# One block table instead of three in a fused attention and expert kernel

## The reference, cut to what matters

```python
# layer 1: attention inside each image, n = 256 positions
q, k, v = wq @ xf + bq, wk @ xf + bk, wv @ xf
sim = softmax(q.T @ k / sqrt(64) + key_mask, axis=2)
x = x + gamma * (sim @ v)
# layer 2: linear attention across the 8 images (cumulative sums over l), on normalized tokens
q, k, v = relu(t @ q_w.T + q_b), relu(t @ k_w.T + k_b), t @ v_w.T + v_b
attn = einsum(q_, cumsum(k_ v)) / max(einsum(q_, cumsum(k_)), 1e-6)
t = t + attn @ out_w.T + out_b
# layer 3: 2048 tokens, 8 experts, each token goes to its best two
probs = softmax(ln(t) @ router_w)          # top 2, weights made to sum to 1
h = silu(x @ w1[e]) * (x @ w3[e])
t = t + sum over the two experts of weight * (h @ w2[e])
```

## Time and profile before

| | us |
|---|---|
| median of 3 runs (lowest, highest) | 198.16 (197.84, 201.89) |
| the profiled execution | 198.26 |
| its span, first to last instruction | 196.5 |
| PE, POOL, DVE, ACT busy | 145.5, 100.4, 100.9, 97.4 |

### The profile page before, as it was taken

The page is one execution under the profiler, slowest core; times in us unless marked ns, Lnnn a source line. Parts: engine busy times, 40 slices in busy tenths (PEclk is TensorE's granted clock), DMA queues, the critical chain, the costliest instruction groups (busy, mean ns, idle before and its releaser), DMA issues.

```text
span 196.5 us, 4178 instructions
## 1 busy us (share of the span) xinstructions
PE 145.5 (74%) x1113; PEld 126.6 (64%) x1113; DVE 100.9 (51%) x400; ACT 97.4 (50%) x294; POOL 100.4 (51%) x142
## 2 busy tenths in 40 slices
PE   1899999999687978763998808866499989892000
PEld 1478886887476756452997808856399979791000
DVE  2177377789329699885156830234045445320163
ACT  3298986878387737131356502433235655552000
POOL 0003340727868688678068777756116746756000
PEclk9999999999969999996699985999889999999555
DMA  6989200000000000139442158661342332110595
GB/s 172 315 251 415 100 2 0 0 3 27 27 29 19 29 27 17 54 96 286 131 126 95 54 142 300 186 203 50 84 95 66 89 77 67 34 42 0 163 273 207
DMA packets 17925, 21.37 MB, mean 109 GB/s; under 512 B 3355, under 2 KB 14304, under 8 KB 17646
## 3 DMA queue, kind: packets, MB, share of 16 engines
q1 hardware_dynamic: 14910, 16.38, 27.8%
q0 software_dynamic: 2272, 4.24, 6.3%
q10 hardware_dynamic: 720, 0.49, 0.9%
HBM read 15.21 MB, written 6.33 MB: 110 GB/s over the span
## 4 chain that ended last, share of the span: by engine, by line
PE 45%; DMA 13%; POOL 12%; issue 11%; SPq 9%; DVE 6%; ACT 2%; POOLq 0%; DVEq 0%; ACTq 0%
PE ps L879 14%; PE ps L894 7%; POOL rows_x L502 6%; DMA xb<-rows_x 4%; PE ps L743 3%; SPq L376 3%; PE ps L723 3%; DMA XT<-rows_y 3%; PE ps L868 2%; DMA rows_x<-pad 2%; PE ps L715 2%; PE ps L708 2%; PE ps L707 2%; PE ps L782 2%; DMA X<-in_x_ch 2%
## 5 line engine op out<-in xcount | busy, mean ns | idle before, releaser
L510 POOL DMA_INDIRECT rows_y<-yb,xb x39 | 38.3, 981 | 27.1 <-ACT yb L661 20.2
L502 POOL DMA_INDIRECT rows_x<-xrow,slot x32 | 36.0, 1125 | 17.8 <-issue 10.8
L879 PE MATMUL ps<-xbT,WB 128*128 128x128 f32 x312 | 42.1, 292 | 0.0
L879 PEld LDWEIGHTS ps<-xbT,WB 128*128 128x128 f32 x312 | 40.6, 210 | 0.0
L894 PE MATMUL ps<-W,hid 128*128 x156 | 25.4, 296 | 5.0 <-DVE hid L1194 3.9
L653 ACT ACTIVATE gate<-ps 128x256 f32<-128x256 f32 x39 | 14.9, 383 | 22.3 <-PE ps L879 19.6
L894 PEld LDWEIGHTS ps<-W,hid 128*128 128x128 f32 x156 | 21.2, 201 | 6.8 <-issue 6.6
L1194 DVE TENSOR_TENSOR hid<-gate,ps 128x256 f32<-128x256 f32 x39 | 16.0, 414 | 18.0 <-ACT gate L653 15.2
L1207 DVE COPY WB<-W 128x512 f32 x22 | 10.2, 462 | 24.5 <-PE ps L879 21.5
L661 ACT ACTIVATE yb<-ps,xb 128x128 f32<-128x128 f32 x39 | 14.4, 368 | 12.6 <-PE ps L894 11.1
L868 PE MATMUL ps<-CF,xb 128*128 128x128 f32 x39 | 9.1, 296 | 11.6 <-DMA xb<-rows_x 10.9
(11 more groups left out here) (141 smaller groups left out, 294.6 us busy)
## 6 DMA issues: line engine op xcount, KB each, us to landing
WB<-in_w SPq DMA_DIRECT2D x17, 256.0 KB, 3.4
xb<-rows_x SPq DMA_DIRECT2D x39, 65.0 KB, 2.0
W<-in_w SPq DMA_DIRECT2D x1, 2048.0 KB, 10.4
X<-in_x_ch SPq DMA_DIRECT2D x8, 128.0 KB, 3.7
XT<-in_x_tok SPq DMA_DIRECT2D x8, 128.0 KB, 3.7
W<-in_w SPq DMA_DIRECT2D x1, 1024.0 KB, 12.5
XT<-rows_y SPq DMA_DIRECT2D x4, 192.0 KB, 4.5
X<-rows_y SPq DMA_DIRECT2D x4, 192.0 KB, 4.6
```

The costliest lines, as they stand in the source:

```text
L502: pool.indirect_dma_start(rows_x, bass.IndirectOffsetOnAxis(ap=slot[:, g:g + 1], axis=0), xrow[:, i * T + t, c, :], None, bounds_check=DUM ...
L510: pool.indirect_dma_start(rows_y, bass.IndirectOffsetOnAxis(ap=xb[:, n, DEST_COL:ROW].bitcast(I32), axis=0), yb[:, n, :], None, bounds_che ...
L879: last = pe.matmul(bank(BANK_GU[s])[:, k * P:(k + 1) * P], WB[:, s % WBS, k * P:(k + 1) * P], xbT[:, s % XBT, :], start=True, stop=True)
```

## The change

- One table of 39 blocks is made after all 8 images are routed. `table_taken`, `pad_lists` and the tables' interleaving go.
- The padding is stored ahead of everything: eight fills of 64 partitions x 8 experts x 520 numbers (1.06 MB each) write every row of all lists. `scatter` of image i waits for fill i.
- `TENSOR_LOAD` of table entries: two at once, of 26 and 13 registers, on each of SP, PE and DVE, ahead of the first block.
- On POOL only the power is left of each norm. The variance plus epsilon (`lin_spread`, `route_spread`) and the negated product (`lin_shift`, `route_shift`) are DVE instructions.
- All 39 blocks' weights are copied by DVE; SP issues no weight loads in the expert part.
- 24 bf16 matmuls of ones on ones stand at the head of PE.
- New written orders on POOL, ACT, PE and DVE: the expert part stands behind all of the front part, and `turn_x`, `gate_up(s + 1)`, `down(s)` alternate singly. New PSUM banks.

```diff
-READ = 8
+READ = 26
+PACK = 4
+WARM_MATMULS = 24
-TABLES = ((4, 9, 0), (6, 8, 9), (8, 22, 17),)
+TABLES = ((8, 39, 0),)
...
+        def read_table(eng, registers, line, k):
+            _, blocks, first = TABLES[k]
+            for s in range(first, first + blocks, READ):
+                m = min(READ, first + blocks - s)
+                eng.reg_load(registers[s:s + m], table[line:line + 1, s:s + m])
...
+            def fill_rows(c):
+                here = rows_x[0:E * CAP, :].rearrange("(e r) d -> e (r d)", e=E)[:, c * N * ROW:(c + 1) * N * ROW]
+                sp.dma_start(here.rearrange("e (p k) -> p e k", k=PACK * ROW),
+                             pad[0:N // PACK, :].unsqueeze(1).broadcast_to([N // PACK, E, PACK * ROW])).then_inc(filled[c], 16)
+            fill_rows(0)
             sp.dma_start(W13[:, :], w13).then_inc(ld_w13, 16)
             sp.dma_start(W2[:, :], w2).then_inc(ld_w13, 16)
+            for c in range(1, B):
+                fill_rows(c)
...
             for k, (_, blocks, first) in enumerate(TABLES):
-                if k == len(TABLES) - 1:
-                    pad_lists()
                 sp.wait_ge(table_done, k + 1)
+                read_table(sp, first_row, T_ROW, k)
...
                 for s in range(first, first + blocks):
                     load_rows(s)
-                    if k < len(TABLES) - 1:
-                        load_weights(s)
...
             def rstd_ffn(i):
                 b = i % 2
-                pool.wait_ge(mv2_done, 2 * (i + 1))
+                pool.wait_ge(ve2_done, i + 1)
                 if i >= 2:
                     pool.wait_ge(xrow_done, 2 * (i - 1))
-                pool.tensor_scalar(nm2[:, b, :], mv2[:, b, :, 0], -1.0, None, ALU.mult)
-                link(pool.tensor_scalar(ve2[:, b, :], mv2[:, b, :, 1], LN_EPS, None, ALU.add))
-                link(pool.tensor_tensor(rs2[:, b, :], ve2[:, b, :], CF[:, C_HALF:C_HALF + T], ALU.pow))
-                pool.tensor_tensor(nb2[:, b, :], nm2[:, b, :], rs2[:, b, :], ALU.mult).then_inc(rs2_done, 1)
+                    pool.wait_ge(nb2_done, i - 1)
+                pool.tensor_tensor(rs2[:, b, :], ve2[:, b, :], CF[:, C_HALF:C_HALF + T], ALU.pow).then_inc(rs2_done, 1)
...
                     pool.wait_ge(dest_ready, 1)
+                    pool.wait_ge(filled[i], 16)
...
+            pe.wait_ge(ones_ready, 1)
+            for _ in range(WARM_MATMULS):
+                pe.matmul(bank(BANK_CV[0])[:, 0:P], ONES[:, :], ONES[:, :], start=True, stop=True)
...
+            def route_spread(i):
+                dv.wait_ge(mv2_done, 2 * (i + 1))
+                dv.tensor_scalar(ve2[:, i % 2, :], mv2[:, i % 2, :, 1], LN_EPS, None, ALU.add).then_inc(ve2_done, 1)
+
+            def route_shift(i):
+                dv.wait_ge(rs2_done, i + 1)
+                if i >= 2:
+                    dv.wait_ge(xrow_done, 2 * (i - 1))
+                dv.scalar_tensor_tensor(out=nb2[:, i % 2, :], in0=mv2[:, i % 2, :, 0], scalar=-1.0, in1=rs2[:, i % 2, :],
+                                        op0=ALU.mult, op1=ALU.mult).then_inc(nb2_done, 1)
```

More of the change, by code:

```diff
@@ L279, in hybrid_block @@
         warm_ready = sem("warm_ready")
-        pool_done = sem("pool_done")
+        ones_ready = sem("ones_ready")
+        filled = [sem(f"filled{c}") for c in range(B)]
+        ve1_done = sem("ve1_done")
+        nb1_done = sem("nb1_done")
+        nb2_done = sem("nb2_done")
         rs1_done = sem("rs1_done")
@@ L358, in pieces @@
             return sum(len(halves(i)) for i in range(n))
-        def table_of(s):
-            return [k for k, (_, _, first) in enumerate(TABLES) if first <= s][-1]
-        def table_reader(eng, line, most):
-            sets = [[eng.alloc_register(f"line{line}_{half}_{n}") for n in range(READ)] for half in range(2)]
-            turn = [1]
-            def read(s):
-                _, blocks, first = TABLES[table_of(s)]
-                n = (s - first) % READ
-                if n == 0:
-                    turn[0] = 1 - turn[0]
-                    m = min(READ, first + blocks - s)
-                    eng.reg_load(sets[turn[0]][0:m], table[line:line + 1, s:s + m])
-                return eng.snap(sets[turn[0]][n], min_val=0, max_val=most)
-            return read
+        def read_table(eng, registers, line, k):
[3 more added lines that the diff above has]
+                eng.reg_load(registers[s:s + m], table[line:line + 1, s:s + m])
         @block.sync
@@ new lines, in _ @@
+            scatter(7, 1); scatter(7, 2); scatter(7, 3); result(0); result(1); result(2); result(3); result(4)
+            result(5); result(6); result(7); result(8); result(9); result(10); result(11); result(12)
+            result(13); result(14); result(15); result(16); result(17); result(18); result(19); result(20)
+            result(21); result(22); result(23); result(24); result(25); result(26); result(27); result(28)
+            result(29); result(30); result(31); result(32); result(33); result(34); result(35); result(36)
@@ L527, in _ @@
+            result(37); result(38)
         @block.scalar
@@ new lines, in _ @@
+            turn_x(21); gate_up(19); down(18); turn_x(22); gate_up(20); down(19); turn_x(23); gate_up(21)
+            down(20); turn_x(24); turn_x(25); gate_up(22); down(21); turn_x(26); gate_up(23); down(22)
+            turn_x(27); gate_up(24); down(23); turn_x(28); gate_up(25); down(24); turn_x(29); gate_up(26)
+            down(25); turn_x(30); gate_up(27); down(26); turn_x(31); turn_x(32); gate_up(28); down(27)
+            turn_x(33); gate_up(29); down(28); turn_x(34); gate_up(30); down(29); turn_x(35); gate_up(31)
@@ L935, in _ @@
+            down(30); turn_x(36); gate_up(32); down(31); turn_x(37); gate_up(33); down(32); turn_x(38)
+            gate_up(34); down(33); gate_up(35); down(34); gate_up(36); down(35); gate_up(37); down(36)
+            gate_up(38); down(37); down(38)
         @block.vector
@@ L1142, in table_rows @@
                 dv.wait_ge(cnt_done, k + 1)
-                if last:
-                    dv.tensor_tensor(pad_row[:, :], cnt[0:1, :], CF[0:1, C_ECAP:C_ECAP + E], ALU.add).then_inc(pad_row_done, 1)
                 link(dv.tensor_scalar(up[:, :], cnt, float(P - 1) if last else 0.0, None, ALU.add))
@@ new lines, in _ @@
+            table_copy(0); read_experts(0); weights(0); weights(1); weights(2); weights(3); weights(4)
+            weights(5); hidden(0); weights(6); hidden(1); weights(7); hidden(2); weights(8); hidden(3)
+            weights(9); hidden(4); weights(10); hidden(5); weights(11); weights(12); hidden(6); hidden(7)
+            weights(13); hidden(8); weights(14); hidden(9); weights(15); hidden(10); weights(16); hidden(11)
+            weights(17); hidden(12); weights(18); hidden(13); weights(19); hidden(14); weights(20); hidden(15)
@@ L1249, in _ @@
+            hidden(38)
             for q in range(PARTS):
```

354 lines of the change are left out of this document (167 added, 187 removed).

## The result

The changed kernel takes 189.92 us (median of 4 runs, 189.45 to 190.78) beside 198.92 us for the kernel before on the same chip (4 runs, 197.84 to 201.89): ratio 0.957, 95% interval 0.950 to 0.964. A second set of six runs gave 189.32 and 0.944 (0.938 to 0.950). Forecast were 187.5 in a range of 181.0 to 196.5, and faster by over 2%.

A forecast was written before the change was run, and what follows sets the result against it. It took PE to bound the kernel until 50 us and from 146 to 178, POOL's spacing from 50 to 92. Terms: 103.6 (last scatter landed) + 64.4 (expert part) + 17.7 (end) + 1.8 (outside span) = 187.5 us; range 181 to 196.5.

The forecast's parts named there:

- first scatter starts: Front part: POOL's first scatter starts at 45.1 us, where it stood at 44.8 before.
- first to last scatter: Front part on POOL: 55.9 us between these starts, with the last scatter starting at 101.
- landed to end of last `down`: Expert part: 39 blocks on PE, with first rows, low clock and gaps, take 64.4 us after the last landing.
- the warm matmuls: Head of PE: 24 matmuls in idle time shorten the slow pace, saving 1.7 us, at worst nothing.
- the new order: Front part on PE: 14 more records stand ahead of the first ranks, adding 2.0 us.
- two DVE waits: After 52 us: waits of 3.6 and 2.4 us, laid to image 5's power behind four scatters, go: -6.0 us.
- DVE stuck behind powers: Front part: DVE's negated products wait for POOL's powers behind 15 scatters; up to 19 us slower, 206.5; chance 0.07.
- the cover that I named: Front part: seven us of DVE work between image 2's slots and image 4's product, against 5.1 + 0.8 needed.
- Register loads at no cost: Before the expert part: loading 39 registers takes 2.6 to 8.7 us, hidden by scatters and landing; charged nothing, at most 1.0.
- Fills at no cost: Front part: eight padding stores on SP's queue finish by 71 us, hidden; late fills cost 15 us, chance 0.04.
- The clock's 2.0 us: Start of the expert part: PE begins at the lower clock after idling, +1.8 us, with first turns +2.0.
- POOL held up by weight copies: Expert part: each DVE copy keeps POOL out for 0.43 us, results take 1.71 each, total 203; chance 0.04.

The follow-up runs named there:

- the last run: Changed kernel with 8 and 14 extra float32 128x128 matmuls put into PE's waits before the first `gate_up`: 191.40 us, ratio 0.952.

## Why the prediction was right, point by point

**What bounds, and in which order.** Held: three stages, POOL's scatters, then PE, and one valley. The forecast of 187.5 was 2.4 under the measured 189.9; the sum's terms, against the profiled execution:

| term | forecast | measured | off |
|---|---|---|---|
| first scatter starts | 45.1 | 48.99 | +3.9 |
| first to last scatter | 55.9 | 56.0 | +0.1 |
| landing | 2.6 | 2.3 | -0.3 |
| landed to end of last `down` | 64.4 | 63.6 | -0.8 |
| end | 17.7 | 17.3 | -0.4 |
| outside the span | 1.8 | 1.9 | +0.1 |

The 2.6 us of these are the miss against 190.09 (the median, 189.92, is 0.2 lower).

**The term that was mis-sized: the first scatter.** I took -1.7 for the warm matmuls and +2.0 for the new order, +0.3 together. Between the two profiled executions the first scatter moved by +4.2, from 44.79 to 48.99, in two parts that the traces separate. From POOL's first power to the first scatter are 27.7 us in both traces of the old order and 29.9 in all ten of the new one with the norms as changed: +2.2, which is the +2.0 of the forecast. The other +2.0 lies ahead of the first power, 17.08 before and 19.09 now, and there a gain of 1.7 was forecast. This part is not settled. The one trace of the kernel before that I read had the earliest head: with the same code ahead of it, the first power came at 19.06 in the run with the power moved. So up to 2 us of the miss is a short slow pace that I took for the rule; against that head the changed kernel's first power is level, and the forecast of an earlier one failed all the same. The new order has a share in it that was not measured: it does the scores of two images first, so that PE then waits for their transposed probabilities.

```profile
15.28 1.16 PE L717 MATMUL ps<-cv,probT 128*128 128x128 f32 x8 [1.60 <-ACT probT L545]
...
19.09 0.72 POOL L451 TENSOR_TENSOR rs<-ve,CF 128x2 f32<-128x2 f32 x1 [12.47 <-DVE ve L991]
```

Of the +2.2, fills are not the cause: it is 29.90 us with half of them and with none. Nor is the norms' move: with the norms back on POOL it is 30.5. That the order is the cause follows by that exclusion; the order alone wasn't run.

**First to last scatter.** 56.0 us beside 55.9, but my way there was only half right, and the hit to 0.1 is luck: with a dip of the clock that some executions have, the same code takes 57.0. Right: POOL's share, and DVE's chains of images 5 to 7 as small additions (0.87, 1.02 and 0.79 us of wait, 2.7 in all and some 1.9 beyond the usual issue, beside my 2). Not shown: that 6.0 us came from two DVE waits; shortening them by 1.1 us in the kernel before brought 0.15. The sum on the way to 55.9 is also off by 0.2 in itself: 84.2 less 2.1 and 6.0, plus 1.8, is 77.9 and not 78.1. What was shown is the price of the instructions taken off POOL, 6.7 us over this stretch.

**Rival: DVE stuck behind powers.** Not in the changed kernel: there DVE's longest wait on a power was 0.7 us. In the old order the same edit meets a wait of 2.86 us and the kernel loses 1.3%, but most of that loss stands ahead of this wait. So the rival's mechanism is seen; what it would cost in the new order without the cover that I named is not.

**Register loads at no cost.** Held, by less than I thought: SP's loads took 4.9 us and were done 1.6 us before the last landing. Of my two bounds, 2.6 and 8.7, neither was the price; 26 registers cost 0.08 us each, the 13 behind them 0.22. The Trainium skill's page "Runtime: NRT & Kernel Launch", section "Instruction fetch mechanics", has about 0.2 us a register, for loads from HBM; the table here lies in SBUF. The 13 agree with it, the 26 don't.

**Fills at no cost.** Held: with half the fills or none, first power to first scatter stays 29.90. They were down by about 62 us, not 71.

**The expert part.** 63.6 beside 64.4. The clock's 2.0 us were 1.9 by the last run. From 122.48 to 157.50 stand 28 results, 1.30 us apart in the mean; behind them they follow PE's pace of 1.45:

```profile
122.48 0.98 POOL L481 DMA_INDIRECT rows_y<-yb,xb  x1 [5.55 <-ACT yb L635]
...
153.49 1.15 POOL L481 DMA_INDIRECT rows_y<-yb,xb  x1 [0.30 <-issue]
...
157.50 0.97 POOL L481 DMA_INDIRECT rows_y<-yb,xb  x1 [0.30 <-issue]
...
161.71 1.01 POOL L481 DMA_INDIRECT rows_y<-yb,xb  x1 [0.44 <-ACT yb L635]
```

**Rival: POOL held up by weight copies.** Fell as a price: 28 results 1.30 us apart with DVE's copies beside them, and 1.28 where DMA brings the weights. Each side does stretch a little: 12 of 39 results took 0.98 to 1.15 us instead of 0.97, and copies up to 0.70 instead of 0.43. The rule of the Trainium skill that I cited ("SBUF — State Buffer", section "SBUF: two separate sides") may be what stretches them, but a result held out for a whole copy, 0.43 us, isn't seen here.

**What I left out.** Moving the weights from DMA to DVE was charged at nothing. It is worth 9 to 13 us against the same one-table kernel with loads, in the one order of SP's queue that was run. The sum came out right since it went by PE's passes at 0.115 us, which holds only if the rows arrive in time; I never asked what 27 loads of 256 KB, and SP standing behind them, would do to them. In the kernel before, the 22 blocks of the third table ran on copies already, so the rows that I read didn't show it.

## What to carry to other kernels

Ask first which queue's spacing, not which engine's busy share, fills a stage: taking three instructions of 0.2 to 0.3 us off GpSimd in each norm was worth 6 us, and only together with an order in which nobody stands behind its powers. Price a part in the kernel in which it will run; the same edit saved 6 us in one and cost 2.5 in the other. Before a place of an event in one trace is taken for a term, look how far it moves in another trace of the same code: here the head alone moved by 2 us. And work put in to keep TensorE going has to end before the data it bridges to arrives: the attempts here ended 5.1 and 3.4 us after the rows, and there were 1.9 us to win.

## What was unexpected of the hardware

- The granted clock stayed at 0.50 while PE was busy without a gap with matmuls of ones (65 rows, bf16, 512 columns) from 108.73 to 115.7. With float32 matmuls of 128x128 from 110.33 on it was 0.50 until 114 and 0.95 in 114 to 116. Twenty-four matmuls of ones at the head of the kernel left the following pairs at 1.06 us too, though the clock's row shows full there. What in the two kinds makes the difference wasn't tried.
- How long that half pace at the head lasts differs from one execution of the same code to the next: until 6.7 to 9.8 us in ten traces, and until 8.9 and 12.4 in two of the kernel before. Whole stages start up to 2 us later by it.
- `TENSOR_LOAD` of 8 table entries took 0.52 to 0.73 us where it began at entry 0, 8, 16 or 24, and 7 entries 1.05; 13 from entry 26 took 2.80, and in the kernel before 8 from entry 9 took 1.74 and 1.80. So an entry costs some 0.07 us in the one case and 0.22 in the other; that the start of the load decides it is the reading that fits all of these, not one that was tried by itself.
- SP was blocked by its own fills: the first issue of 1.06 MB took 0.72 us, the next seven 29.15.

```profile
9.68 0.72 SPq L387 DMA_DIRECT2D rows_x<-pad  x1
...
12.58 29.15 SPq L387 DMA_DIRECT2D rows_x<-pad  x7
```

Nothing else stood in SP's queue for that time, so it cost nothing here.
